# Nine gate sums added up on TensorE, and the first weighted product taken pass by pass

## The reference, cut to what matters

```python
def _binary_diff_weight(w, base):
    d = w - base
    coeff = jnp.mean(jnp.abs(d))
    return base + coeff * jnp.sign(d)
W1, W2, W3 = ...              # gate, down, up; each 1792 x 512, one coeff each
gate = xn @ W1.T
up = xn @ W3.T
f = (silu(gate) * up) @ W2.T
```

## Time and profile before

| | us |
|---|---|
| median of 3 runs (534.46, 534.47, 535.68) | 534.47 |
| the profiled execution, whole | 534.48 |
| its span, first to last instruction | 532.7 |
| TensorE busy in it | 519.8 |
| VectorE busy | 443.0 |
| ScalarE busy | 328.5 |
| GpSimd busy | 94.6 |

### The profile page before, as it was taken

How to read it: one execution, slowest core, us unless ns; L and a number is a source line. 1 busy time by engine, 2 the same in 40 slices (tenths; PEclk the granted TensorE clock), 3 DMA queues, 4 the chain that set the end, 5 groups by cost and what they waited for, 6 DMA issues and landing times.

```text
span 532.7 us, 6530 instructions
## 1 busy us (share of the span) xinstructions
PE 519.8 (98%) x2352; PEld 432.1 (81%) x2352; DVE 443.0 (83%) x520; ACT 328.5 (62%) x455; POOL 94.6 (18%) x106
## 2 busy tenths in 40 slices
PE   4999999999999999999999999999999999999997
PEld 3778888888888888888888888888888888888886
DVE  6989998988896988865898888999999898874447
ACT  2979978557546655446648557968776585464310
POOL 1311002003100310022003121300310040004491
PEclk9999999999999999999999999999999999999999
DMA  8999905045711491059228994941592387127503
GB/s 337 394 401 404 385 8 168 15 137 98 197 54 46 76 234 49 1 106 223 56 70 160 250 217 90 186 101 40 109 187 47 74 163 144 36 46 161 135 20 139
DMA packets 31745, 76.73 MB, mean 144 GB/s; under 512 B 3873, under 2 KB 7297, under 8 KB 31585
## 3 DMA queue, kind: packets, MB, share of 16 engines
q1 hardware_dynamic: 21632, 57.42, 34.4%
q0 software_dynamic: 9792, 18.88, 20.5%
q10 hardware_dynamic: 288, 0.02, 0.0%
HBM read 53.23 MB, written 2.10 MB: 104 GB/s over the span
## 4 chain that ended last, share of the span: by engine, by line
PE 95%; DVE 3%; DMA 1%; issue 0%; ACT 0%; SPq 0%
PE up_ps L1726 28%; PE gate_pair L1726 27%; PE down_pair L1767 11%; PE up_ps L1767 9%; PE down_ps L1767 7%; PE side_ps L1810 2%; PE down_pair L1726 2%; PE down_pair L1677 1%; PE up_ps L1887 1%; PE gate_pair L1887 1%; PE down_pair L1887 1%; DMA xn<-in_x 1%; PE down_pair L1849 1%; PE gate_pair L1767 1%; PE down_pair L1782 1%; DVE xn L1135 1%
## 5 line engine op out<-in xcount | busy, mean ns | idle before, releaser
L1726 PE MATMUL up_ps<-xT,gu 128*128 128x512 f32 x648 | 151.9, 390 | 0.0
L1726 PE MATMUL gate_pair<-xT,gu 128*128 128x512 f32 x624 | 148.4, 390 | 0.9 <-DVE gu L1175 0.9
L1726 PEld LDWEIGHTS up_ps<-xT,gu 128*128 128x128 f32 x648 | 121.6, 188 | 25.1
L1726 PEld LDWEIGHTS gate_pair<-xT,gu 128*128 128x128 f32 x624 | 117.2, 188 | 25.4 <-DVE gu L1175 1.4
L655 POOL DMA_DIRECT2D y<-y_part x64 | 55.4, 878 | 338.3 <-ACT y_part L819 337.1
L806 ACT ACTIVATE h<-up_ps 128x512 fp32r<-128x512 f32 x52 | 31.1, 597 | 110.1 <-DVE up_ps L1242 57.0
L865 ACT ACTIVATE ramp<-codes,bend_bias 128x1536 f32<-128x1536 uint8 x56 | 88.1, 1580 | 1.9 <-DVE acc L1350 1.6
L1350 DVE SCALAR_TENSOR_TENSOR acc<-ramp,acc 128x1536 f32<-128x1536 f32 x42 | 73.6, 1753 | 4.9 <-ACT ramp L865 4.3
L1767 PE MATMUL down_pair<-h,dn 128*128 128x512 f32 x249 | 60.9, 390 | 0.0
L1767 PEld LDWEIGHTS down_pair<-h,dn 128*128 128x128 f32 x249 | 46.8, 188 | 9.8
L1247 DVE TENSOR_TENSOR h<-up_ps,h 128x512 fp32r<-128x512 f32 x52 | 35.8, 688 | 19.7 <-ACT h L806 19.4
(11 more groups left out here) (227 smaller groups left out, 647.2 us busy)
## 6 DMA issues: line engine op xcount, KB each, us to landing
y<-y_part POOLq DMA_DIRECT2D x64, 256.0 KB, 5.1
scale<-in_scales SPq DMA_DIRECT2D x28, 384.0 KB, 5.5
scan_w<-in_w SPq DMA_DIRECT2D x15, 512.0 KB, 11.0
base<-in_mean SPq DMA_DIRECT2D x9, 768.0 KB, 4.4
scan_mean<-in_mean SPq DMA_DIRECT2D x9, 512.0 KB, 10.1
silu_gate<-in_mean SPq DMA_DIRECT2D x6, 512.0 KB, 12.4
codes<-in_codes SPq DMA_DIRECT2D x14, 192.0 KB, 6.0
xn<-in_x SPq DMA_DIRECT2D x4, 512.0 KB, 5.0
```

The source lines that it names most:

```text
L1726: last = nc.tensor.matmul(ps[:, :], w[:, w_part, hc * P:(hc + 1) * P], xT[:, x_part, hc, th * HALF:(th + 1) * HALF], start=(hc == 0 and w_ ...
```

## The change

`total(GATE)` is replaced by `total_gate`: TensorE multiplies each of the nine columns by the ones matrix and accumulates them in one PSUM column. The ones matrix holds 1/(INTER*HID) now, so the sum is the coefficient. `split_make` reads it from PSUM; `keep_coeff` copies it for the others. The early products go pass by pass, `split_low` in halves becomes one `unit_low`, and `project_split` takes all high-weight passes before the low ones. Waits and places in four queues move; `AGAIN` and `WARM_LOW` go, `WARM_TOTAL` comes.

```diff
-AGAIN = 3
-WARM_LOW = {1: 6, 2: 5, 3: 5}
+WARM_TOTAL = [5, 8]
...
-            nc.gpsimd.memset(ones[:], 1.0).then_inc(const_ready, 1)
+            nc.gpsimd.memset(ones[:], 1.0 / (INTER * HID)).then_inc(const_ready, 1)
...
             def early_low():
                 pool.wait_ge(gu_hi, 1)
-                pool.wait_ge(scan_diff, dve_tiles(1))
...
             early_low()
+            pool.wait_ge(scan_diff, dve_tiles(1))
             unit_subtract(0)
-            pool.wait_ge(xT_lo, 4)
             unit_subtract(1)
...
             x_high(3)
+            early_high()
             scan_signs(0)
-            early_high()
             x_high(4)
...
             unit_signs(3)
+            scan_signs(4)
             silu(0, 0)
             silu(0, 1)
-            scan_signs(4)
             silu(1, 0)
+            unit_high(3)
             scan_signs(5)
-            unit_high(3)
             next_gate_high()
...
+            def keep_coeff(m):
+                dve.wait_ge(total_ready, m + 1)
+                nc.vector.tensor_copy(coeff[:, m:m + 1], side_ps[:, m:m + 1]).then_inc(coeff_ready, 1)
+
             def take_coeff(m):
-                dve.wait_ge(total_ready, m + 1)
-                nc.vector.tensor_scalar(coeff[:, m:m + 1], side_ps[:, m:m + 1], 1.0 / (INTER * HID), None, ALU.mult
-                                        ).then_inc(coeff_ready, 1)
+                keep_coeff(m)
                 dve.wait_ge(coeff_ready, m + 1)
...
                 dve.wait_ge(unit_sign, SPLIT_UNIT + 1)
+                dve.wait_ge(total_ready, GATE + 1)
                 nc.vector.scalar_tensor_tensor(unit_base(SPLIT_UNIT)[:, sl], unit_raw(SPLIT_UNIT)[:, sl],
-                                               coeff[:, GATE:GATE + 1], unit_base(SPLIT_UNIT)[:, sl], ALU.mult, ALU.add
+                                               side_ps[:, GATE:GATE + 1], unit_base(SPLIT_UNIT)[:, sl], ALU.mult, ALU.add
                                                ).then_inc(half_made if half == 0 else unit_made, 1)
...
             for t in range(4, TT):
                 normalise(t)
+            x_low(0)
+            x_low(1)
             scan_subtract(1)
-            for t in range(4):
+            for t in range(2, HC):
                 x_low(t)
...
             scan_sum(4)
-            take_part(GATE)
-            take_coeff(GATE)
             split_make(0)
             split_make(1)
-            split_low(0)
-            split_low(1)
+            keep_coeff(GATE)
+            unit_low(SPLIT_UNIT)
+            dve.wait_ge(coeff_ready, 1)
             early_scale(0)
             unit_make(2)
-            early_add(0)
             early_scale(1)
             unit_low(2)
+            scan_subtract(5)
+            early_add(0)
             early_add(1)
-            scan_subtract(5)
             unit_make(3)
...
+            def early_pass(th, w_part, x_part):
+                if w_part == LO:
+                    pe.wait_ge(gu_lo, 1)
+                elif x_part == LO:
+                    pe.wait_ge(xT_lo, TT // 2 * (th + 1))
+                else:
+                    pe.wait_ge(gu_hi, 1)
+                    pe.wait_ge(xT_lo, th + 1)
+                    pe.wait_ge(xT_hi, TT // 2 * (th + 1))
                 for hc in range(HC):
+                    nc.tensor.matmul(early_ps[th][:, :], gu_weight(0, GATE)[:, w_part, hc * P:(hc + 1) * P],
+                                     xT[:, x_part, hc, th * HALF:(th + 1) * HALF],
+                                     start=(hc == 0 and w_part == x_part == HI), stop=(hc == HC - 1 and x_part == LO))
...
             def early_signs(th):
                 pe.wait_ge(unit_sign, 1)
                 for hc in range(HC):
-                    if th == 1 and hc == 2:
-                        total(GATE)
...
+            def total_gate():
+                sum_wait(pe, SCAN_TILES - 2)
+                pe.wait_ge(unit_abs, FIRST - 1)
+                for n in [*range(SCAN_TILES - 1), *range(SCAN_TILES, SUMS - 1)]:
+                    nc.tensor.matmul(side_ps[:, GATE:GATE + 1], ones[:], abs_sums[:, n:n + 1], start=(n == 0), stop=False)
+                pe.wait_ge(unit_abs, FIRST)
+                nc.tensor.matmul(side_ps[:, GATE:GATE + 1], ones[:], abs_sums[:, SUMS - 1:SUMS], start=False, stop=False)
+                sum_wait(pe, SCAN_TILES - 1)
+                nc.tensor.matmul(side_ps[:, GATE:GATE + 1], ones[:], abs_sums[:, SCAN_TILES - 1:SCAN_TILES],
+                                 start=False, stop=True).then_inc(total_ready, 1)
...
+            def project_split():
+                w = gu_weight(SPLIT_UNIT, GATE)
+                for hc in range(HC):
+                    if hc == 0:
+                        pe.wait_ge(half_hi, 1)
+                    if hc == HC // 2:
+                        pe.wait_ge(gu_hi, SPLIT_UNIT + 1)
+                    for x_part in (HI, LO):
+                        nc.tensor.matmul(gate_bank(SPLIT_UNIT, 0)[:, :], w[:, HI, hc * P:(hc + 1) * P],
+                                         xT[:, x_part, hc, 0:HALF], start=(hc == 0 and x_part == HI), stop=False)
+                pe.wait_ge(gu_lo, gu_count(SPLIT_UNIT, GATE))
+                for hc in range(HC):
+                    last = nc.tensor.matmul(gate_bank(SPLIT_UNIT, 0)[:, :], w[:, LO, hc * P:(hc + 1) * P],
+                                            xT[:, HI, hc, 0:HALF], start=False, stop=(hc == HC - 1))
+                last.then_inc(gate_done, 1)
...
-            early_mean(0)
+            for th in range(2):
+                early_pass(th, HI, HI)
+                early_pass(th, LO, HI)
+            early_pass(0, HI, LO)
             early_signs(0)
-            early_mean(1)
+            early_pass(1, HI, LO)
             early_signs(1)
-            for c in range(1, FIRST + 1):
+            warm(gate_ps[1], WARM_TOTAL[0])
+            total_gate()
+            warm(gate_ps[1], WARM_TOTAL[1])
+            project_split()
+            project(SPLIT_UNIT, GATE, 1)
+            for c in range(SPLIT_UNIT + 1, FIRST + 1):
```

More of the change, by code:

```diff
@@ L362, in block_kernel @@
         half_hi = sem("half_hi")
-        half_lo = sem("half_lo")
         early_part = sem("early_part")
@@ L1660, in _ @@
                 pe.wait_ge(xn_ready, t + 1)
[L1661 to L1664, removed]
+                for c in range(HC):
+                    last = nc.tensor.matmul(x_ps[t][:, c * P:(c + 1) * P], xn[:, t, c * P:(c + 1) * P], ident[:],
+                                            is_transpose=True, start=(c == 0), stop=(c == HC - 1))
                 last.then_inc(xT_tr, 1)
@@ L1667, in _ @@
                     warm(side_ps, WARM[t])
[L1668 to L1674, removed]
-                for hc in range(HC):
[L1676 to L1680, removed]
+            def early_pass(th, w_part, x_part):
[7 more added lines that the diff above has]
+                    pe.wait_ge(xT_hi, TT // 2 * (th + 1))
+                for hc in range(HC):
+                    nc.tensor.matmul(early_ps[th][:, :], gu_weight(0, GATE)[:, w_part, hc * P:(hc + 1) * P],
+                                     xT[:, x_part, hc, th * HALF:(th + 1) * HALF],
+                                     start=(hc == 0 and w_part == x_part == HI), stop=(hc == HC - 1 and x_part == LO))
             def early_signs(th):
@@ L1693, in total @@
             def total(m):
-                pe.wait_ge(part_ready, m + 1)
+                pe.wait_ge(part_ready, m)
                 nc.tensor.matmul(side_ps[:, m:m + 1], ones[:], abs_part[:, m:m + 1], start=True, stop=True
                                  ).then_inc(total_ready, 1)
+            def total_gate():
[8 more added lines that the diff above has]
+                                 start=False, stop=True).then_inc(total_ready, 1)
             def project(k, kind, th, total_within=None):
-                if k == SPLIT_UNIT and kind == GATE and th == 0:
-                    pe.wait_ge(half_lo, 1)
-                elif kind == GATE or k <= FIRST:
+                if kind == GATE or k <= FIRST:
                     pe.wait_ge(gu_lo, gu_count(k, kind))
@@ L1722, in project @@
                 for hc in range(HC):
-                    if hc == HC // 2 and k == SPLIT_UNIT and kind == GATE and th == 0:
-                        pe.wait_ge(gu_lo, gu_count(k, kind))
                     for w_part, x_part in PASSES:
```

## The result

The changed kernel takes **537.05 us** (median of six, 536.49 to 537.74) against 534.47: a ratio of 1.0045, 95% interval 1.0035 to 1.0055. By the medians it is slower by 2.6 us. The forecast was 535.4, the range ended at 536.9, and slower by over 0.3% had been given a chance of 0.14. So the loss at `total(UP)` was forecast and came; the split unit lost 0.73 us where nothing was forecast; and the whole is 2.6 us where 0.9 had been said. The median lies 0.15 us outside the range; the ratio, put on 534.47, gives 536.9, its very end.

A forecast was written before the change was run, and what follows sets the result against it. TensorE was taken as the bound, busy 519.8 of 532.7 us, its split product set by the gate coefficient's chain. 534.5 plus 0.0 at the split unit and 0.9 at total(UP) gave 535.4 us, range 533.8 to 536.9.

The forecast's parts named there:

- the loss at `total(UP)`: At the UP total in TensorE's stream, a stall of 1.0, or 0.9 us with favourable fractions, because ScalarE is late.
- the split unit: At the first split product: it starts at 31.34 against 31.36 before, a change of 0.0 us.
- The sum on TensorE: At the gate coefficient: 18 one-column matmuls 0.11 us apart make split_make start at 30.34 against 29.91, 0.43 later.
- the gain of the split unit's part: Between split_make and the split product: 1.00 us instead of 1.45, since the high passes need no low half.
- TensorE before the sum: Ahead of the sum: low part starts near 15.9, first high pass at 17.8; early work ends at 27.6, not 30.41.
- What is late next: Behind split_make: early_add(0) 6.31 us after it, ScalarE 1.5 late, UP part's result at 50.8, stall 0.9 at total(UP).
- What the order alone would do: At total(UP): the stall is 0.4 us if scan_subtract(5) takes 1.21 like others of its kind.
- The sum of the terms: Whole kernel: 0.0 at the split unit plus 0.9 at total(UP) on 534.5, giving 535.4 us.
- The clock rival: Behind the coefficient sum the clock falls, matmuls at 0.45 instead of 0.227, costing 1.5 to 2.6 us; chance 0.12.
- The quick rival: At the coefficient sum: matmuls 0.07 to 0.08 apart and ScalarE catching up, time 533.6 to 534.7 us; chance 0.28.
- the serial accumulation: At the coefficient sum: matmuls 0.25 us each, product 1 starts 2.4 later, time 537 to 538; chance 0.05.

The follow-up runs named there:

- run 1: The changed kernel with GpSimd's low part of unit 0 waiting for the last normalised tile; 536.03 us.
- run 6: The kernel before with early_high ahead of the signs of tile 0 and GpSimd's low part of unit 0 right behind it; 535.70 us.
- run 3: The changed kernel with the sum as before: VectorE adds the nine columns, TensorE makes one total; fill kept; 536.08 us.
- run 9: The changed kernel with the edits of run 1 and run 3, keeping the change's own order behind the coefficient; 534.18 us.
- run 4: The changed kernel with the edits of run 1, run 2 and run 3 together; 534.21 us, ratio 0.9997 to the kernel before.
- run 7: run 4 with GpSimd's subtraction of unit 4 put behind scan_subtract(5); 534.20 us.
- run 11: run 4 with ScalarE's scan_signs(4) ahead of unit_high(2), and unit_sum(4) and unit_high(3) ahead of scan_signs(5); 533.61 us.
- run 2: The changed kernel with ScalarE's and VectorE's order behind the coefficient put back as before; 536.5 us.
- run 10: The changed kernel with the single total and without the 5 and 8 transposes of fill; 536.16 us.
- run 5: The changed kernel without its 5 and 8 transposes of fill around the sum; 537.72 us.

## Why the prediction was right and where it was wrong

*The sum on TensorE*: right, once its start is put right. In run 1, where GpSimd is out of the way, the first wide matmul is at 17.77 (forecast 17.8), `split_make` at 30.37 (30.34), the split product at 31.36 (31.34). The earlier trace rows have only the 0.32 of the two matmuls of a total; that the second starts 0.07 behind the first and lasts 0.25 stands in the trace, not in them. The pace was 0.107 for 0.11, the scalar from PSUM cost nothing (0.89 for two halves, 0.88 in the earlier trace rows), and the gain of the split unit's part was 0.45 as priced (0.99 from `split_make` to product).

*TensorE before the sum* is the step that failed. It moved the low part to 15.9 and asked only when it would be ready, not what ran on VectorE meanwhile. Its price is 0.96 us on four normalised tiles, 0.74 at `scan_sum(4)` (28.21 for 27.47) and 0.73 at the split product. Runs 1 and 6 show it from both sides.

*What is late next*: the place and size of the wait were right (1.0 or 0.9 at `total(UP)`, measured 1.09), the way to it only in part. `early_add(0)` was forecast 6.31 us behind `split_make` and the result of `take_part(UP)` 20.5; measured are 6.68 and 20.7, which is the other 0.3. The forecast took over the 1.64 of `scan_subtract(5)` from the earlier trace rows without asking why it is longer than the 1.21 of its kind. It is a meeting with GpSimd's unit 4 already there:

```profile
34.55 1.47 POOL L641 TENSOR_TENSOR unit_st<-unit_st 128x512 f32<-128x512 f32 x1 [9.89 <-DMA unit_st<-in_mean]
```

In the changed kernel `scan_subtract(5)` comes behind it and takes 1.22, and `unit_make(2)` is hit instead, for 0.85. That is read from the trace: no run moves unit 4 in the changed kernel itself. Its data also landed at 33.5 there, against 34.5 or 34.6 before and in runs 1 and 3, and why is not known. What the order alone would do had been forecast too, a stall of 0.4 with a `scan_subtract(5)` of 1.21; run 9 has 1.22 and 0.38.

*The sum of the terms* for the profiled execution: 0.9 forecast, 0.73 and 0.3 missed, 1.9 to 2.0; measured 2.07 (536.55 less 534.48). The 2.6 of the medians has the executions with the lower clock in it, which no term of the sum held.

*The clock rival*, at 0.12: half of the executions have a lower mean clock, at 1.1 us where 1.5 to 2.6 was asked. That it fell at the sum is not shown, as no profile of the changed kernel caught it, but the counts point there. Run 3 differs from the changed kernel only in the sum, and has a clock below 0.999 in none of six. With the single total and the fill there is none in 50 (runs 3, 4, 7, 9, 11), with nine columns and the fill three of six, one of nine (run 1) and one of five (run 2), with the single total and no fill four of six (run 10), with nine columns and no fill six of six (run 5). Run 5's profile has a fall behind the thin stretch near 17 us too, so that place stays possible. The prediction read the low clock at 11.07 us from durations alone (0.24 us a transpose for 0.118); the granted clock of the profile from 7.6 to 12.9 us is 1.00, so that level is inferred.

*The quick rival and the serial accumulation* are both refuted by 0.107.

## What to carry to other kernels

An operation on GpSimd that is set free early is not free of charge: look at what VectorE runs in that window, and count a meeting as a cost on whichever of the two starts second. Adding up the parts of a sum early gains only if the engine that does it is idle before the last part is ready, and quicker than what it replaces: nine columns at two matmuls each cost 1.93 us of TensorE to save a VectorE operation of 0.16 us and its handover. Costs undone one at a time need not add up: here they gave 0.5, 0.0 and 0.4 us apart and 2.3 together. And follow a gain to the next point at which the bound engine must wait: here what was won at the split product was decided 18 us later, at a sum that ScalarE fed.

## What the runs showed of the hardware that was not expected

VectorE and GpSimd slow each other, but not for all operations. Beside a GpSimd operation with two SBUF inputs, four normalising operations went from 1.91 to 2.87, a scalar_tensor_tensor from 0.74 to 1.59 or 1.78, a subtraction of two SBUF tiles from 1.21 to 2.32. Subtractions with one input in PSUM were not slowed: in run 1 two of them (x tiles against PSUM) take 1.28 beside GpSimd's low part, and 1.27 in the changed kernel, where GpSimd was idle then. When VectorE had started first, GpSimd took 2.08 for 1.30.

The ends of the operations show how: the one that starts second goes on only when the first has ended, and then takes nearly its full time. A VectorE operation of 0.7 us ends 0.55 us behind GpSimd's end (35.33 behind 34.78 in the changed kernel, 36.28 behind 35.72 in run 10), one of 1.2 us ends 1.08 behind it (37.39 behind 36.31 in run 1, 37.16 behind 36.08 in run 4), and GpSimd's of 1.3 us ends 1.15 behind VectorE's (36.68 behind 35.53 in run 9, 38.41 behind 37.26 in run 7), however much of the first was left when they met. So a meeting costs what is left of the first operation when the second starts.

The Trainium skill, page "GPSIMD Engine Reference", section "Specifications", states that the two engines share the SBUF interfaces, with contention for VectorE instructions in a two-port mode or with two SBUF inputs. The rows agree for the operations with two SBUF inputs. The normalising operation has one, and no row shows in which mode it runs.
